# A fused decoder layer on one core: full-height matmuls cut into half-height pairs, PSUM banks handed out in twos

## The reference

```
x = LN(x + A(x));  x = LN(x + X(x));  x = LN(x + F(x))
A: h = LN(x)*g + b; 4 heads of 64; p = relu(h @ w_fc_head^T)^2; x + p @ w_proj_head       (w_fc, w_proj as 1024 x 64)
X: 16 heads of 16; softmax(gamma*(QK^T/4) + delta*(ap*max(D,0) + an*min(D,0))) @ V, then Wo
   D = clip(frac_k - frac_q, -0.2, 0.2); K and V from ctx; with biases
F: top-1 of 8 experts by x @ gate_W^T + gate_b; relu(x @ wi^T + wi_b + lora_e(x)) @ wo^T + wo_b   (256 -> 1024 -> 256)
```

## Time and profile before

| | |
|---|---|
| median of 3 runs | 866.87 us |
| profiled execution | 868.24 us, its span 866.4 us |
| TensorE matmul busy | 824.3 us (95%), 8444 matmuls |
| TensorE weight loads busy | 594.3 us (69%) |
| VectorE / ScalarE / GpSimd busy | 720.1 (83%) / 704.0 (81%) / 581.2 us (67%) |
| granted TensorE clock | full (2.4 GHz), but for a few slices at the page's 0.8 to 0.9; mean 0.987 |
| DMA | 46.32 MB, mean 53 GB/s |
| chain that ended last | PE 84%, DVE 5%, ACT 4%, issue 2%, POOL 2% |

### The profile page before, as it was taken

How to read it: one execution, slowest core, us unless ns; L and a number is a source line. 1 busy time by engine, 2 the same in 40 slices (tenths; PEclk the granted TensorE clock), 3 DMA queues, 4 the chain that set the end, 5 groups by cost and what they waited for, 6 DMA issues and landing times.

```text
span 866.4 us, 23427 instructions
## 1 busy us (share of the span) xinstructions
PE 824.3 (95%) x8444; PEld 594.3 (69%) x8444; DVE 720.1 (83%) x2148; ACT 704.0 (81%) x1930; POOL 581.2 (67%) x754
## 2 busy tenths in 40 slices
PE   7889899999999999999999999999999999999896
PEld 6545556767777676767767676676768667667686
DVE  5887988887888888888888888888888887889854
ACT  3658998897888989798897979888898988888841
POOL 5677878675777868586786768678776867543511
PEclk9998999999999999999999999999999999999899
DMA  7233222222131213223122312313231321323100
GB/s 170 99 65 69 50 56 44 42 40 56 44 62 44 56 38 57 45 52 67 44 57 44 68 26 60 59 45 61 50 63 20 64 55 32 62 45 56 32 14 25
DMA packets 38149, 46.32 MB, mean 53 GB/s; under 512 B 10417, under 2 KB 27313, under 8 KB 38034
## 3 DMA queue, kind: packets, MB, share of 16 engines
q1 hardware_dynamic: 38034, 44.82, 26.0%
HBM read 15.42 MB, written 4.19 MB: 23 GB/s over the span
## 4 chain that ended last, share of the span: by engine, by line
PE 84%; DVE 5%; ACT 4%; issue 2%; POOL 2%; SPq 1%; DMA 1%; POOLq 0%; DVEq 0%; ACTq 0%
PE bank L308 12%; PE bank L503 12%; PE bank L295 11%; PE bank L256 10%; PE bank L421 8%; PE bank L435 7%; PE bank L405 4%; PE bank L381 4%; PE bank L362 2%; PE bank L328 2%; PE bank L342 2%; PE bank L513 2%; PE bank L387 2%; ACT P L711 1%; DVE T L939 1%
## 5 line engine op out<-in xcount | busy, mean ns | idle before, releaser
L1165 POOL TENSOR_TENSOR R<-R 128x512 f32<-128x512 f32 x208 | 220.4, 1063 | 74.8 <-ACT R L655 74.4
L711 ACT ACTIVATE P<-T,NM 128x256 f32<-128x256 f32 x512 | 256.9, 512 | 13.0 <-DVE NM L939 12.9
L1183 POOL TENSOR_SCALAR U<-DP,alph 128x512 f32<-128x512 f32 x256 | 188.1, 736 | 108.5 <-DVE NM L939 72.8
L930 DVE SCALAR_TENSOR_TENSOR bank<-DN,alph,bank 128x512 f32<-128x512 f32 x256 | 180.2, 749 | 47.3 <-PE bank L405 47.1
L939 DVE CUSTOM_DVE_ANT_0 T<-bank,U 128x256 f32<-128x256 f32 x512 | 185.9, 419 | 2.4 <-POOL U L1183 1.3
L655 ACT ACTIVATE R<-bank 128x512 f32<-128x512 f32 x248 | 134.0, 597 | 30.9 <-PE bank L295 29.2
L633 ACT ACTIVATE STG<-bank 128x512 f32<-128x512 f32 x256 | 138.5, 596 | 13.9 <-PE bank L421 12.5
L308 PE MATMUL bank<-R,VS 128*32 128x512 f32 x992 | 120.6, 602 | 6.2 <-DVE R L884 3.8
L295 PE MATMUL bank<-SK,KH 64*128 64x512 f32 x480 | 107.4, 443 | 5.7 <-ACT XO L655 2.4
L711 ACT ACTIVATION_READ_ACCUMULATOR P<-T,NM 128x1 f32 x512 | 103.6, 202 | 0.0
L421 PEld LDWEIGHTS bank<-ident,P 64*128 64x128 f32 x2048 | 77.1, 140 | 36.4 <-issue 27.7
(11 more groups left out here) (180 smaller groups left out, 1826.2 us busy)
## 6 DMA issues: line engine op xcount, KB each, us to landing
QS<-QK SPq DMA_DIRECT2D x384, 64.0 KB, 2.3
XG<-in_x SPq DMA_DIRECT2D x16, 256.0 KB, 3.0
CT<-in_ctxT SPq DMA_DIRECT2D x16, 256.0 KB, 2.9
out<-XO SPq DMA_DIRECT2D x15, 256.0 KB, 2.5
FK<-in_frac SPq DMA_DIRECT2D x16, 128.0 KB, 3.2
STG<-in_wiT SPq DMA_DIRECT2D x2, 512.0 KB, 5.5
STG<-in_woT SPq DMA_DIRECT2D x2, 512.0 KB, 4.3
STG<-in_kT SPq DMA_DIRECT2D x2, 256.0 KB, 4.1
```

What stands on the lines that cost most here:

```text
L711: eng.activation(P[n % NP][:, cs], T[n % NT][:, cs], ACT.Exp, bias=NM[:, n % 8, q:q + 1], scale=-1.0, accum_out=SU[n // 16 % 2][:, q, seat ...
L930: eng.scalar_tensor_tensor(out=L[:, :], in0=dn[:, :], scalar=alph[:, 16 + h:17 + h], in1=L[:, :], op0=ALU.mult, op1=ALU.add).then_inc(s_t1, 1)
L1165: eng.tensor_tensor(r, r, r, ALU.mult).then_inc(s_sqp, 1)
L1183: eng.tensor_scalar(U[n % NU][:, :], dp[:, :], alph[:, h:h + 1], 0.0, ALU.mult, ALU.add).then_inc(s_u, 1)
```

## The change

1. Row heights. All full-height products become half-height ones: a product with 128 rows is two matmuls of 64 rows (phase 0 and phase 1). Two results, x and y, in two banks are made side by side: in phase 0 x gets rows 0 to 63 and y rows 64 to 127, in phase 1 the other way round. Phase 1 waits for the end of phase 0 (`s_half`) and has a place of its own. `kp` and `vp` become one such pair (`kp_vp`), `qp`, `op`, `gate` and each two of `ffn_in`, `low_rank`, `ffn_out` too. The 128x128 transposes become pairs of 64x128 ones, whose results lie in two banks and are read interleaved (`woven`). Only `av`, `values` (and `bias_o`, once) stay at full height.
2. Banks. The four ring banks and the two of the logits become three pairs. `lease` gives a call the pair that is expected free first, by a table of hold times in places (`LEASE`); the choice is fixed when the program is written out. The logits lease a pair as well.
3. `ao` writes its result back into the leased pair of `rcT`, and `aoh` and `aol` read it there; `AO` goes, `rx` writes `RX` and no longer waits for `aol` but for `rcT`. The pair of `rcT` is free at `s_aol` instead of `s_rb`.
4. The gate chain has six instructions in place of seven: compare and multiply are fused into scalar_tensor_tensor.
5. `on_dve` is true only in blocks 0 and 1: 14 x 2 squares move to POOL. `y1` is two instructions of 256 elements.
6. The fillers are half-height transposes, and every place on every engine has a new number.

```
-        psum = [ctx.enter_context(nc.psum_tensor(f"bank{i}", [128, 512], f32)) for i in range(8)]
-        pL, pV, pA = psum[4:6], psum[6], psum[7]
+        turf = ctx.enter_context(nc.psum_tensor("turf", [128, 6, 512], f32))
+        psum = [turf[:, k, :] for k in range(6)]
...
         def on_dve(b, u):
-            return u % 8 == 7 or (b < 2 and u % 2 == 1)
+            return b < 2 and u % 2 == 1
...
+        LEASE = {"lg": 37, "turn": 5, "sc": 25, "fi": 73, "fo": 128, "kp": 50, "qp": 51, "op": 44, "gate": 54,
+                 "gsT": 25, "uT": 13, "xnT": 13, "otT": 16, "x1T": 18, "rcT": 15, "x2T": 16, "bo": 307}
+        def lease(*names):
+            p = min(range(3), key=lambda q: (expected[q], q))
+            expected[p] = max(expected[p], moment[0]) + LEASE[names[0][0]]
+            before, tenant[p] = tenant[p], names
...
+            return [psum[2 * p], psum[2 * p + 1]], before or ()
...
+            def products(x, y, terms, phase, fresh):
+                for n, (lx, rx, ly, ry) in enumerate(terms):
+                    eng.matmul(x, lx[half(phase), :], rx[half(phase), :], start=(fresh and n == 0), stop=False,
+                               skip_group_check=True)
+                    end = eng.matmul(y, ly[half(1 - phase), :], ry[half(1 - phase), :], start=(fresh and n == 0),
+                                     stop=False, skip_group_check=True)
+                return end
...
             def xnT(b):
-                bank, before = take("xnT", b)
-                bank_free(before)
+                banks = two("xnT", b)
...
-                        i = eng.transpose(bank[:, hp * 256 + t * 128:hp * 256 + t * 128 + 128],
-                                          XN[:, t, hp * 128:hp * 128 + 128], ident[:, :])
+                        for j in range(2):
+                            o = hp * 128 + t * 64
+                            i = eng.transpose(banks[j][:, o:o + 64], XN[half(j), t, hp * 128:hp * 128 + 128],
+                                              ident[half(j), half(j)])
...
+            def ffn_in(b, v):
+                u, phase = v // 2, v % 2
+                if phase == 0:
+                    two("fi", b, 2 * u)
...
+                else:
+                    pe.wait_ge(s_half["fi"], 2 * b + u + 1)
...
             def logits(p):
-                pe.wait_ge(s_tt, 4 * p)
+                pL = two("lg", 0, 2 * p)
...
             def ao(b):
-                eng.tensor_tensor(AO[:, :, :], pV[:, :].rearrange("p (g t) -> p g t", g=2), RB[:, :, :],
+                scaled = both("rcT", b)[:, :, 0:256]
+                eng.tensor_tensor(scaled, pV[:, :].rearrange("p (g t) -> p g t", g=2), RB[:, :, :],
...
-                for b, u in due(g, 1309, 4, 29, early=-19, late=239):
+                for b, u in due(g, 1301, 4, 19, early=1, late=499):
                     ffn_in(b, u)
-                for b, u in due(g, 1426, 8, 24, early=-1, late=2067):
+                for b, u in due(g, 1495, 4, 38, early=1, late=622):
                     ffn_out(b, u)
-                for b, _ in due(g, 1179, early=-22, late=349):
-                    gate(b)
+                for b, u in due(g, 1168, 2, 22, early=-70, late=-166):
+                    gate(b, u)
```

More of the change, by code:

```diff
@@ L247, in _, with banks_free, two @@
             pe = Port(eng)
-            def bank_free(before):
-                if before is not None:
-                    s, v = released(*before)
+            def banks_free(before):
+                for tenancy in before:
+                    s, v = released(*tenancy)
                     pe.wait_ge(s, v)
[L254 to L258, removed]
+            def two(name, b, i=0):
+                banks, before = lease((name, b, i), (name, b, i + 1))
+                banks_free(before)
+                return banks
+            def products(x, y, terms, phase, fresh):
[5 more added lines that the diff above has]
+                return end
             def bias_o():
                 v = stage(512, 2).rearrange("p (a b) -> p a b", a=2)
-                bank, before = take("bo", 0)
-                bank_free(before)
+                bank, _ = two("bo", 0)
                 pe.wait_ge(d_w["o"], STAGED["o"][1])
@@ L285, in scores @@
                 cs = slice(c * 128, c * 128 + 128)
[L286 to L290, removed]
+                banks = two("sc", b, 2 * c)
                 pe.wait_ge(s_wlo["kT"], 1 + c // 4)
@@ L312, in otT @@
             def otT(b):
-                bank, before = take("otT", b)
-                bank_free(before)
+                banks = two("otT", b)
                 pe.wait_ge(s_ot, b + 1)
@@ L409, in turn @@
             def turn(p):
-                banks = []
-                for j in range(2):
-                    bank, before = take("turn", 0, 2 * p + j)
-                    bank_free(before)
-                    banks.append(bank)
+                banks = two("turn", 0, 2 * p)
                 pe.wait_ge(s_ex, 4 * p + 4)
@@ L440, in rcT @@
             def rcT(b):
-                bank, before = take("rcT", b)
-                bank_free(before)
+                banks = two("rcT", b)
                 pe.wait_ge(s_rx, b + 1)
@@ L506, in low_rank @@
-            def low_rank(b, f2):
-                bank = bank_of["fi", b, f2]
-                pe.wait_ge(s_ull, b + 1)
-                pe.wait_ge(s_wlo["lb"], 1)
-                pe.wait_ge(d_lb, 32)
-                for i in range(2):
-                    cs = slice((2 * f2 + i) * 128, (2 * f2 + i) * 128 + 128)
-                    m = eng.matmul(bank[:, i * 256:i * 256 + 256], LB[:, cs], UL[:, :], start=False, stop=True,
-                                   skip_group_check=True)
-                m.then_inc(s_fi, 1)
+                banks = two("uT", b)
@@ L537, in filler @@
+                end = products(x, y, terms, int(piece in (1, 2)), piece == 0)
+                if piece % 2 == 0:
+                    end.then_inc(s_half["fo"], 1)
+                elif piece == 3:
+                    end.then_inc(s_fo, 1)
             def filler(count, bank):
-                for _ in range(count):
-                    eng.matmul(bank[:, 0:128], ident[:, :], ident[:, :], start=True, stop=True)
+                for _ in range(2 * count):
+                    eng.transpose(bank[:, 0:64], ident[half(0), :], ident[half(0), half(0)])
```

689 lines of the change are left out of this document (342 added, 347 removed).

## The result

The changed kernel takes 895.25 us (median of 4 runs, 893.14 to 895.83), the kernel before 866.53 in the same job (864.42 to 867.24): ratio 1.0317, 95% interval 1.0279 to 1.0354. I had predicted 832, range 803 to 862. It is slower, and outside the range. The profiled execution took 895.83 us, its span 894.0. Of all the runs behind this text one was in the slow state (1487 us, in experiment 12); the ratios are of the fast ones.

What follows compares the result with a forecast made beforehand. PE's own stream was taken to bound the middle: a 50.0 us block - 3.4 - 0.95 + 0.3 = 45.9, +2.0 for banks = 47.9. Over 14.7 blocks that saves 31 us, plus 3 behind: 832 us, range 803 to 862.

Steps and rivals of the forecast that it cites:

- Products at 0.12 a pair: On PE, 152 full-height matmuls a block become 152 half-height pairs at 0.12 us either way: no change.
- Phases, +0.3: On PE, phase 1 waiting for the end of phase 0 costs 0.3 us a block, only in `gate`.
- Changes of height and transposes, -4.35: On PE, 19 fewer changes of height save 3.4 us a block, five half-height transposed tiles 0.95.
- The 45.9: PE's forecast us a block before added bank waits: 50.0 - 3.4 - 0.95 + 0.3, old stall included.
- the old stall: PE's 0.85 us standstill a block in the kernel before, from the last scores pair to the turn.
- Banks, +2.0: PE's waits for leased pairs: 1.6 + 1.4 = 3.0 us a block minus the 0.85 stall, taken as +2.0.
- the walks: Calls laid end to end against the three pairs' holds: 1.6 us of waits a block at least, 8.4 at most.
- The walk with shortest holds: The lower end: five leases a block come too early, around `rcT`, `otT`, first `ffn_out` and `gate`: 1.6 us.
- banks decide: Rival: bank waits at `turn`, `otT` and first `ffn_out` behind `rcT` make the kernel slower, 885 us; chance 0.10.
- The tail, -7: From scores(15, 0) to the end: 3 us less behind 800 us and 4 less for the 1.8 blocks before.
- ACT or DVE binds: Rival: ACT keeps 5.5 of its 6.5 idle us, block 49.0 us, 851 us in all; chance 0.17.
- the span forecast: The whole kernel: 34 us less, 31 from 14.7 blocks at 2.1 us each and 3 behind 800 us.

Runs made afterwards that it cites:

- experiment 12: Kernel before with only the gate chain fused (six DVE instructions in place of seven): 865.04 us against 867.18, ratio 0.9973.
- Experiment 9: Changed kernel with all projection and feed-forward products full-height again, places, leases and phases kept: 926.49 us, ratio 1.0656 to the kernel before.
- experiment 3: Changed kernel with `ao` writing to SBUF again and the pair of `rcT` free at `s_rb`: 896.12 us.
- experiment 10: Changed kernel with ACT copying only 256 of 512 columns of each turned bank from block 3 on: 872.92 us.
- experiment 2: Kernel before with `otT`, `x1T`, `x2T`, `rcT` made half-height in two neighbouring banks of the ring of four: 926.77 us.
- experiment 5: Changed kernel with the first DVE instruction on the logits writing to SBUF, so their pair is free at `s_t1`: 910.62 us.

## Why the prediction was wrong

- *Products at 0.12 a pair*: right, 0.118.
- *Phases, +0.3*: right in size. Only `gate` pays in the middle (0.21). In the last block phases of `low_rank`, `ffn_in`, `ffn_out` and `op` stand right behind each other and pay 0.22 each.
- *Changes of height and transposes, -4.35*: too much. Take the waits off both periods: before 49.96 - 0.62 (0.85 of the earlier trace rows less 0.23) = 49.3; after 50.5 - 4.67 = 45.8, phases included. That is 3.5 us less, where the sum had -3.4 - 0.95 + 0.3 = -4.05. Experiment 9 says which term: a change costs 0.12 us there, and 0.15 if the whole difference is put on the 19 counted, not 0.18. I had read 0.20 off three rows and used it for twelve changes. The 45.9 looked right only because the old stall was still inside it.
- *Banks, +2.0*: the step that failed. Waits of 2.6 us a block in all (2.0 and the old 0.6) were forecast, 4.67 were there. A slip is part of it: the walks gave 3.0, and I took 0.85 off for the old stall, of which by my own reading 0.62 was wait, and rounded down. The walk with shortest holds named `otT`, the first `ffn_out` and `gate` rightly, but gave them too little: it freed a scores' pair 2.1 us after the call, while from the call (420.16) to `otT` (423.01) it is 2.85, with ACT's `OT` and exponentials in front. It missed `kp_vp`, `gsT` and `ffn_in`. And 1.4 us were put on the turn behind `rcT`, where 0.16 is waited (experiment 3: nothing to gain there).
- *The threshold* of the rival "banks decide" was 4.1 us beyond the old stall. The measured 4.67 - 0.62 = 4.05, with 0.5 us of the work term missing, makes the block 0.5 us longer than before. That rival, at 885 us and a chance of 0.10, was the right one. Of the places that it named, `otT` and the first `ffn_out` have the longest waits and the `turn` hardly any. The reason that it gave, `aol` behind a `biased` in DVE's queue, was not there: most of the waits end with the copies and relus of ACT.
- *The clock* was no term of the sum. Three middle blocks have a granted clock of 0.97 and take 52.0 us: 4.5 us of the 11.5. Before, none from 210 to 710 us had. In experiment 10, with 1.2 us less of waits a block, they are gone. Waits alone do not bring them, though: experiment 2 has 4.7 us of idle time in each block of 54.5 and a clock of 1.00 through ten blocks:
```profile
203.00:757.00 554.00, 505.75 (x5434) 362.31 (x5432) 432.07 (x1354) 444.84 (x1221) 369.83 (x477) 1.00 0.25 48
```
So what makes the clock fall stays open. A forecast for a kernel that is bound by TensorE should still have a term for it, here 1.5 us for each block that it strikes.
- *The tail, -7*: +18. PE is idle 27.0 instead of 17.2 us there and busy 8.2 us longer, at a clock of 0.92 instead of 0.97. An estimate from these clocks: 0.08 x 174.6 = 14 us of clock are missing, where 0.03 x 156.6 = 5 were, which is about what PE is busy longer; why the clock is lower there is open. Two things can be seen. Without scores between them the logits and turns of the last block follow each other closely and lease pair after pair (waits of 2.6, 1.8 and 1.2 us), where before the logits had two banks to themselves. And scores calls stand 82 places apart instead of 73: the last of block 15 comes 44.8 us after the first instead of 38.5, and all that follows in that block hangs on it. How the waits divide between leases and places was not tried: experiment 10 takes away 5.
- *ACT or DVE binds*: no, both still wait for PE over the block, though ACT is the one that lets go of the pairs.

By numbers, of the 61.6 us between the span forecast (866.4 - 34 = 832.4) and 894.0: in the twelve blocks of the middle 12 x (50.5 - 47.9) = 31, of which 25 are waits and 6 work, and 4.5 of clock; in the tail 18 + 7 = 25. The head came out as forecast within 1 us.

## What to carry to other kernels

- Occupation (84% was reckoned; by the holds of the changed kernel, some 130 us in 3 x 50.5, it was 86%) says little about a set of buffers that is leased in a fixed order. Walk the order, and for the n-th call behind a lease ask whether the engine has more work in between than the reader needs from its own queue: three pairs and scores, logits, turn in a row leave 1.2 us for 1.1 us of relu plus whatever ACT does first.
- A gain on the bounding engine is real only while its buffers come free at the new pace. Here half-height products save 31 us (experiment 9), and the kernel is still 29 us slower: waits that the old rings did not have, the clock and the tail took more. Whether a better order of the calls would bring the waits down, or three pairs are too few for any order, no run tells.
- Take the old stall out before adding up terms, or it hides an error of its own size.

## What was not expected of the hardware

- DVE and POOL hold each other up where DVE reads SBUF alone. The reduce with accumulator, 128x256, took 420 ns with one input in PSUM beside any POOL instruction. With both inputs in SBUF it took 419 ns alone and up to 1504 beside POOL's tensor_tensor; POOL's `U` went from 704 to 859 ns in the mean (experiment 5). A multiply of 16 elements a row took 0.17 us alone and 0.73 beside POOL (experiment 12).
- A DVE instruction with a single tensor in SBUF is held up too. The `differences`, over the whole run, first before, then after:
```profile
L918 DVE TENSOR_SCALAR DN<-FK,fT 128x256 f32<-128x256 f32 x32 | 10.8, 378 | 0.0
```
```profile
L924 DVE TENSOR_SCALAR DN<-FK,fT 128x256 f32<-128x256 f32 x32 | 26.0, 852 | 0.0
```
They cost DVE 15 us more at their new place. The traces say what goes with it. Before, 31 of the 32 run while POOL does nothing and take 340 to 348 ns, and the one beside POOL takes 1414. After, three run without POOL (337 to 350 ns) and 29 beside its tensor_tensor (491 to 1447 ns). A block of each, two of them in one row, first after, then before, where POOL does nothing from 446.0 to 447.9 us:
```profile
402.80 1.28 POOL L1163 TENSOR_TENSOR XN<-XN,bB 128x512 f32<-128x512 f32 x1
403.75 1.54 DVE L924 TENSOR_SCALAR DN<-FK,fT 128x256 f32<-128x256 f32 x2
404.04 1.09 POOL L1168 TENSOR_TENSOR R<-R 128x512 f32<-128x512 f32 x1
```
```profile
446.71 0.60 DVE L918 TENSOR_SCALAR DN<-FK,fT 128x256 f32<-128x256 f32 x2
```
- Blocks of one and the same order took 50.5 us at a granted clock of 1.00 and 52.0 at 0.97, nine and three of twelve.
